# Selective-scan stage on one core: later split of B, B products and decays issued further ahead, one more decay buffer

## The chip, the cores and the metric

One NeuronCore of a Trainium2 chip runs the whole kernel. The metric is device time in microseconds (us) for one execution; lower is better. The engines are named as in the profile: PE is TensorE (matmuls), DVE is VectorE, ACT is ScalarE, POOL is GpSimd and SP is the engine that issues most DMAs.

## What is computed

The program is a Mamba block (layer norm, input projection, short convolution, selective scan in both directions, gate, output projection) on 4 images of 96 channels and 1024 positions, followed by a windowed-attention block with an MLP. The change is in the first part. Cut to what it touches:

```python
dbl = xr @ W_xproj
dt = jax.nn.softplus(dbl[..., :DT_RANK] @ W_dt + b_dt)
Bm = dbl[..., DT_RANK:DT_RANK + D_STATE]
Cm = dbl[..., DT_RANK + D_STATE:]
A = -jnp.exp(A_log)
def step(h, inp):
    dt_t, B_t, C_t, x_t = inp
    h = jnp.exp(dt_t[:, :, None] * A) * h + (dt_t * x_t)[:, :, None] * B_t[:, None, :]
    y_t = jnp.einsum('ben,bn->be', h, C_t)
    return (h, y_t)
```

There are 192 inner channels, 16 states, 1024 steps and 8 sequences (4 images in 2 directions).

## The kernel before, in words

The (sequence, channel) pairs fill 12 tiles of 128 partitions. Each tile has 16 **units**, one for each state, so the stage has 192 units, and unit k is state k mod 16 of tile k // 16. A unit takes these steps, each on a [128, 1024] fp32 array:

- ScalarE makes the decay `a = exp(dt*A)` (`decay(k)`, L620) into a ring of `A_RING` buffers.
- B of this state is spread over the channels. For 165 units TensorE does it with matmuls into PSUM (`spread_b`, L421), and VectorE multiplies the result by `u = dt*x` (`times_b`, L789). For the 27 units of `POOL_UNITS` a DMA replicates B into `b_rep`, GpSimd multiplies it by `u` (`b_product`, L759), and ScalarE copies the product to PSUM (`copy_b`, L630).
- VectorE runs the recurrence over the 1024 steps (`scan`, L802).
- GpSimd multiplies the states by C, which a DMA has replicated (`read_out`, L749, result `hc`).
- TensorE adds `hc` into the tile's output in PSUM by an identity matmul (`sum_states`, L451), three units later (`SUM_LAG`).

Every engine runs its own program in order; semaphores join them. The program of an engine is a loop over k, and at each k it also does what `front(k)` finds in the hand-written table `PLAN`: projections and convolutions for later tiles (jobs `conv`, `xp`, `dt`, `z`, `cen`, `var`, `out`), each with the unit at which TensorE issues it. TensorE has two PSUM banks `f_ps` for these jobs, so a job waits until ScalarE has emptied the bank of the job two before it. In step k TensorE spreads B for unit k + 1, then does `front(k)`, then sums unit k - 3. ScalarE in step k does `copy_b(k + 1)`, `decay(k + 2)` and `front(k)`; its copy and its decay of a step both wait for the scan of unit k - 1. GpSimd in step k does `b_product(k + B_AHEAD)`, `read_out(k)` and `front(k)`. The scan of unit k waits for the state product of unit k - 4, since the ring of states has four buffers.

The projection `xp` gives B and C for one sequence. B is needed by TensorE as three bf16 terms that add up to the fp32 value. They are made in a relay between two engines: ScalarE rounds to the high term (L543), GpSimd subtracts it (`rest`, L694), ScalarE rounds the remainder to the middle term (`middle`, L550 and L551), and GpSimd subtracts again (`lowest`, L700). There are eight sequences, of which one is split before the loop. The `dt` job has a relay as well: ScalarE takes four passes (`softplus`), then GpSimd does four operations in four successive units (`soft_lost`, `soft_more`, `soft_sum`, `dt_times_x`, L705 to L718). For images 2 and 3 the norm has one too: ScalarE, GpSimd (`scale_norm`, L686), ScalarE (`affine`, L518).

Of the kernel before, what the change touches and what calls it, by code (L numbers as in the profile page):

```python
# [18 lines left out]
E_LO, E_HI = 128, E_IN - 128  # L19
PAIR_ROWS = E_HI  # L20
LN_EPS = 1e-5
A_RING, H_RING, HC_RING, C_RING, SUM_LAG = 3, 4, 4, 4, 3
ROWS = 3 * 2 * N_ST + RANK
LOADS = [4, 7, 12, 8]

# [26 lines left out]
def cols(th, n=HALF):  # L52
# [38 lines left out]
SEQS = [j[1:3] for j in JOBS if j[0] == "xp" and j[3] == 0]  # L91
POOL_UNITS = (4, 18, 22, 36, 38, 46, 51, 53, 65, 68, 80, 83, 97, 99, 113, 117, 126, 130, 136, 147, 153, 163, 165, 177,
              181, 185, 189)
B_RING, B_AHEAD, B_LOAD = 2, 3, 3


def groups_of(b):
# [34 lines left out]
def mamba(nc, t, x1, early, bn_stats, bc_d):  # L132

    with ExitStack() as ctx:
        def sb(name, shape, dt=F32):
            return ctx.enter_context(nc.sbuf_tensor(name, shape, dt))
# [22 lines left out]
        var = sb("var", [C, L])  # L159
# [332 lines left out]
        def _(act):  # L492
# [17 lines left out]
            def variance_left(b, th):  # L510
                leave(("var", b, th), var[:, cols(th)], bank("var", b, th)[0:C, :], ACT.Ln, bias=norm[:, 2:3])
                if th == 1:
                    left(act, J("var", b, 1))
                    nc.scalar.activation(var[:, :], var[:, :], ACT.Exp, scale=-0.5).then_inc(inverse, 1)
# [6 lines left out]
            def conv_left(tile, th):  # L521
                if th == 0 and tile in XR_BEFORE:
                    act.wait_ge(summed, N_ST * XR_BEFORE[tile] + SKIP_UNIT + 2)
                leave(("conv", tile, th), xr_of(tile)[:, cols(th)], bank("conv", tile, th),
                      bias=conv_b[:, kind_of(tile):kind_of(tile) + 1])

            def silu(tile):
                left(act, J("conv", tile, 1))
                nc.scalar.activation(xr_of(tile), xr_of(tile), ACT.Silu).then_inc(xr_ready, 1)

            def xp_left(b, d, th):
                slot = seq_slot(b, d)
                if b >= 2 and th == 0:
                    act.wait_ge(c_stored[slot], 16)
                    act.wait_ge(st_done, SEQS.index((b - 2, d)) + 1)
                    act.wait_ge(job_done, J("dt", tile_of("H", 0, d), 1))
                leave(("xp", b, d, th), dbc[:, slot, cols(th)], bank("xp", b, d, th)[0:ROWS, :], ACT.Copy)
                if th == 1:
                    left(act, J("xp", b, d, 1))
                    act.dma_start(bc_d[2 * b + d], dbc[0:2 * N_ST, slot, :]).then_inc(c_stored[slot], 16)  # L540
                    if b >= 2:
                        act.wait_ge(spread, products_before(N_ST * (tile_of("H", 0, d) + 1)))
                    nc.scalar.activation(st[:, slot, :], dbc[0:ROWS - RANK, slot, :], ACT.Copy).then_inc(st_high, 1)  # L543

            def middle(b, d):
                slot, i = seq_slot(b, d), SEQS.index((b, d))
                act.wait_ge(st_rest, i + 1)
                if i:
                    act.wait_ge(st_done, i)
                nc.scalar.activation(st[64:96, slot, :], dbc[64:96, slot, :], ACT.Copy).then_inc(st_mid, 1)  # L550
                nc.scalar.activation(mid[0:32, :], dbc[0:32, slot, :], ACT.Copy).then_inc(st_mid, 1)  # L551

            def dt_left(tile, th):
                kind = kind_of(tile)
                if th == 0:
                    if tile:
                        act.wait_ge(soft, 4 * tile)
                    if tile >= 2:
                        act.wait_ge(exp_done, N_ST * (tile - 1))
                act.wait_ge(job_done, J("dt", tile, th))  # L560
                nc.scalar.activation(dt[:, tile % 2, cols(th)], bank("dt", tile, th), ACT.Relu,
                                     bias=b_dt[:, kind:kind + 1])
                nc.scalar.activation(t3[:, cols(th)], bank("dt", tile, th), ACT.Abs, bias=b_dt[:, kind:kind + 1])\  # L563
                    .then_inc(left_act, 1)
# [21 lines left out]
            def front(k):  # L586

                for at, name, *job in PLAN:
                    done = DONE_AT[(name, *job)]
                    if done == k and name == "conv":  # L590
                        conv_left(*job)
                        if job[1] == 1:
                            silu(job[0])
                    if done == k and name == "xp":
                        xp_left(*job)
                    if done + 2 == k and name == "xp" and job[2] == 1:
                        middle(*job[0:2])
                    if done == k and name == "dt":
                        dt_left(*job)
                    if done + 1 == k and name == "dt" and job[1] == 1:  # L600
                        softplus(job[0])
                    if done == k and name == "cen":
                        center_left(*job)
                    if done == k and name == "var":
                        variance_left(*job)
                    if done + 3 == k and name == "var" and job[1] == 1:
                        affine(job[0])
                    if done == k and name == "z":
                        z_left(*job)

            def decay(k):

                if k >= UNITS:
                    return
                tile, n = divmod(k, N_ST)
                if n == 0:
                    act.wait_ge(soft, 4 * tile + 3)
                if k >= A_RING:
                    act.wait_ge(scanned, k - A_RING + 1)
                nc.scalar.activation(a[:, k % A_RING, :], dt[:, tile % 2, :], ACT.Exp,  # L620
                                     scale=a_neg[:, kind_of(tile), n:n + 1]).then_inc(exp_done, 1)
# [51 lines left out]
            silu(1)  # L673
            nc.scalar.preload_act_table_set("natural_log_exp_and_others")
            act.wait_ge(set_up, 5)
            for k in range(2):
                decay(k)
            for k in range(UNITS):
                copy_y(k)
                copy_b(k + 1)  # L680
                decay(k + 2)
                front(k)

        def scale_norm(engine, eng, b):
# [35 lines left out]
        @block.gpsimd  # L720
        def _(pool):
            def front(k):

                for at, name, *job in PLAN:
                    done = DONE_AT[(name, *job)]
                    if name == "xp" and job[2] == 1:
                        if done + 1 == k:
                            rest(nc.gpsimd, pool, SEQS.index(tuple(job[0:2])))
                        if done + 2 == k:
                            lowest(nc.gpsimd, pool, SEQS.index(tuple(job[0:2])))  # L730
                    if name == "dt" and job[1] == 1:
                        if done + 2 == k:
                            soft_lost(nc.gpsimd, pool, job[0])
                        if done + 3 == k:
                            soft_more(nc.gpsimd, pool, job[0])
                        if done + 4 == k:
                            soft_sum(nc.gpsimd, pool, job[0])
                        if done + 5 == k:
                            dt_times_x(nc.gpsimd, pool, job[0])
                    if name == "var" and job[1] == 1 and done + 1 == k:  # L740
                        scale_norm(nc.gpsimd, pool, job[0])

            def read_out(k):

                pool.wait_ge(scanned, k + 1)
                pool.wait_ge(c_in[k % C_RING], 16 * c_loads(k))
                if k >= HC_RING:
                    pool.wait_ge(summed, k - HC_RING + 1)
                nc.gpsimd.tensor_tensor(hc[:, k % HC_RING, :], h[:, k % H_RING, :], c_rep[:, k % C_RING, :],  # L749
                                        ALU.mult).then_inc(hc_done, 1)  # L750

            def b_product(k):

                if k not in POOL_UNITS:
                    return
                i, tile = POOL_UNITS.index(k), k // N_ST
                pool.wait_ge(soft, 4 * (tile + 1))
                pool.wait_ge(b_in[i % B_RING], 16 * b_loads(i))
                nc.gpsimd.tensor_tensor(b_rep[:, i % B_RING, :], b_rep[:, i % B_RING, :], u[:, tile % 2, :],  # L759
                                        ALU.mult).then_inc(b_times_u, 1)  # L760

            for k in range(UNITS):
                b_product(k + B_AHEAD)
                if k < UNITS - 1:
                    read_out(k)
                front(k)
# [694 lines left out]
```

## Time and profile before

| | |
|---|---|
| time, median of 3 runs | 1193.46 us (1192.46 to 1195.16) |
| the profiled execution's own time | 1198.2 us |
| its span | 1196.4 us |
| busy over the span: PE, DVE, ACT, POOL | 90%, 77%, 48%, 77% |
| mean granted clock of TensorE | 0.944 of full speed |
| busy from 100 to 200 us: PE, DVE, ACT, POOL | 95.50, 93.59, 71.81, 98.33 us |

The units run from 60 to 750 us; the attention block fills the rest. Busy time counts an instruction from its start to its end, and neighbours on one engine overlap a little, so a row's mean is slightly longer than the step from one start to the next. In a timeline the bracket at the end of a row is the time that the engine stood idle before it, and what ended that.

### The profile page before, as it was taken

The page shows a single profiled execution, that of the slowest core. Times are in us where ns is not written, and L with a number is a line of the kernel's source. Part 1 is how long each engine was busy: PE and PEld are TensorE (multiplying, and loading weights), DVE is VectorE, ACT ScalarE, POOL GpSimd, SP SyncE. Part 2 cuts the span into 40 slices and gives each one's busy share as a digit, 9 for nine tenths or more (in the row PEclk, how much of TensorE's full clock was granted, in tenths as well). Part 3 has the DMA queues.
Part 4 walks back from the last instruction along what each step waited for, and adds up shares of the span by engine and source line. Part 5 has one row for each costly group of instructions (what it writes and reads, how often), then busy time and mean ns, then how long its engine had stood idle before and what let it go on. Part 6 is the DMA issues. An engine that isn't in the chain of part 4 may idle for free. (4 is left out here: it accounts for less than half of the span.)

```text
span 1196.4 us, 9538 instructions
## 1 busy us (share of the span) xinstructions
PE 1073.9 (90%) x3268; PEld 376.1 (31%) x3268; DVE 920.1 (77%) x598; ACT 572.2 (48%) x601; POOL 919.3 (77%) x371
## 2 busy tenths in 40 slices
PE   7889999799998999998987979699999999997675
PEld 2223333233333333333332323233333333332221
DVE  1299998779998899998989899400587796969871
ACT  5766858697777654867675644211121121011311
POOL 0089999979998979998999998100298877989880
PEclk8879999899999999999998999699999999998787
DMA  3234566544475545664546474343938476473402
GB/s 84 93 127 157 178 179 158 186 134 157 163 191 146 176 145 147 173 199 154 169 169 176 129 224 157 83 104 73 201 74 184 89 171 116 116 132 58 91 0 75
DMA packets 111042, 165.65 MB, mean 138 GB/s; under 512 B 63411, under 2 KB 76441, under 8 KB 110993
## 3 DMA queue, kind: packets, MB, share of 16 engines
q1 hardware_dynamic: 108880, 157.81, 48.9%
q10 hardware_dynamic: 2112, 7.23, 2.1%
q8 instruction: 26, 0.43, 0.1%
q14 instruction: 24, 0.19, 0.1%
HBM read 137.43 MB, written 11.23 MB: 124 GB/s over the span
## 5 line engine op out<-in xcount | busy, mean ns | idle before, releaser
L749 POOL TENSOR_TENSOR hc<-h,c_rep 128x1024 f32<-128x1024 f32 x191 | 447.5, 2359 | 103.4 <-DVE h L802 91.3
L802 DVE TENSOR_TENSOR_SCAN h<-a,bu 128x1024 f32<-128x1024 f32 x192 | 436.9, 2284 | 32.9 <-ACT bu L630 10.0
L451 PE MATMUL y_ps<-hc,ident 128*128 128x512 f32 x768 | 378.4, 617 | 0.8 <-DVE hc L850 0.3
L620 ACT ACTIVATE a<-dt,a_neg 128x1024 f32<-128x1024 f32 x192 | 216.5, 1143 | 132.1 <-DVE h L802 126.9
L1231 POOL TENSOR_TENSOR prod_p<-vw,at 128x3584 f32<-128x3584 f32 x18 | 130.4, 7242 | 122.8 <-DMA vw<-v_d 116.9
L789 DVE TENSOR_TENSOR bu<-bu,u 128x1024 f32<-128x1024 f32 x165 | 199.7, 1210 | 21.9 <-PE bu L421 21.7
L451 PEld LDWEIGHTS y_ps<-hc,ident 128*128 128x128 f32 x768 | 144.5, 195 | 202.9 <-issue 182.1
L1112 PE MATMUL sc_ps<-x,w_up 128*64 128x512 f32 x672 | 177.9, 604 | 1.2 <-DMA x<-qk 1.2
L1112 PE MATMUL sc_ps<-x,w_low 96*64 96x512 f32 x672 | 177.5, 603 | 0.0
L1182 ACT ACTIVATE sc<-sc_ps,rel 128x512 f32<-128x512 f32 x24 | 16.5, 688 | 257.4 <-PE sc_ps L1112 257.4
L421 PE MATMUL bu<-st,pick 96*128 96x512 bf16 (+1 forms) x438 | 101.7, 390 | 37.8 <-DVE h L802 36.3
L1238 POOL TENSOR_TENSOR prod_p<-prod_p 128x1536 f32<-128x1536 f32 (+1 forms) x36 | 104.6, 2905 | 2.8
L1317 DVE TENSOR_REDUCE e_ps<-at 128x32 f32<-128x1568 f32 x6 | 17.5, 2921 | 98.1 <-DMA at<-scores_d 98.1
L1231 DVE TENSOR_TENSOR prod_v<-vw,e_ps 128x3584 f32<-128x3584 f32 (+1 forms) x24 | 86.8, 3616 | 0.5
L1337 DVE TENSOR_TENSOR acc_ps<-acc_ps,prod_v 128x1024 f32<-128x1024 f32 x66 | 81.3, 1232 | 2.3
L1112 PEld LDWEIGHTS sc_ps<-x,w_up 128*64 128x64 f32 x672 | 49.6, 137 | 101.4 <-issue 101.4
L1112 PEld LDWEIGHTS sc_ps<-x,w_low 96*64 96x64 f32 x672 | 49.8, 136 | 98.7 <-issue 98.7
L329 PE MATMUL f_ps<-xn,w_taps 96*128 96x512 f32 x128 | 70.4, 653 | 7.4 <-ACT t L563 5.2
L421 PEld LDWEIGHTS bu<-st,pick 96*128 96x128 bf16 (+1 forms) x438 | 26.7, 103 | 155.9 <-DVE h L802 84.4
L759 POOL TENSOR_TENSOR b_rep<-b_rep,u 128x1024 f32<-128x1024 f32 x27 | 63.6, 2357 | 2.8 <-DMA b_rep<-bc_d 2.8
L1128 PE MATMUL g_ps<-x,c_w 96*128 96x512 f32 x48 | 33.3, 855 | 25.5 <-DVE x L1309 25.5
L1204 ACT ACTIVATE up<-g_ps,c_b 128x512 f32<-128x512 f32 x24 | 16.5, 687 | 70.9 <-PE g_ps L1128 70.9
(130 smaller groups left out, 992.6 us busy)
## 6 DMA issues: line engine op xcount, KB each, us to landing
c_rep<-bc_d SPq DMA_DIRECT2D x128, 512.0 KB, 4.0
c_rep<-bc_d SPq DMA_DIRECT2D x128, 256.0 KB, 4.1
vw<-v_d SPq DMA_DIRECT2D x24, 532.0 KB, 9.1
x<-qk SPq DMA_DIRECT2D x66, 171.0 KB, 5.3
b_rep<-bc_d SPq DMA_DIRECT2D x17, 512.0 KB, 5.0
b_rep<-bc_d SPq DMA_DIRECT2D x20, 256.0 KB, 5.2
scores_d<-sc ACTq DMA_DIRECT2D x24, 196.0 KB
at<-scores_d SPq DMA_DIRECT2D x24, 196.0 KB, 3.4
```

The lines of the kernel that those rows point to most:

```text
L329: mm = pe.matmul(out, w_taps[:, j, 0:E_LO], xn[:, i, s:s + HALF], start=(j == 0), stop=(j == TAPS - 1))
L421: mm = pe.matmul(bu[rows, k % 2, cols(th)], pick[:, n:n + 1].to_broadcast([ROWS - RANK, rows.stop - rows.start]), st[:, seq_slot(b, d), co ...
L451: mm = pe.matmul(y_ps[:, cols(th)], ident[:, :], hc[:, k % HC_RING, cols(th)], start=(n == 0 and d == 0), stop=(n == N_ST - 1))
L620: nc.scalar.activation(a[:, k % A_RING, :], dt[:, tile % 2, :], ACT.Exp, scale=a_neg[:, kind_of(tile), n:n + 1]).then_inc(exp_done, 1)
L749: nc.gpsimd.tensor_tensor(hc[:, k % HC_RING, :], h[:, k % H_RING, :], c_rep[:, k % C_RING, :], ALU.mult).then_inc(hc_done, 1)
L759: nc.gpsimd.tensor_tensor(b_rep[:, i % B_RING, :], b_rep[:, i % B_RING, :], u[:, tile % 2, :], ALU.mult).then_inc(b_times_u, 1)
L789: nc.vector.tensor_tensor(bu[:, k % 2, :], bu[:, k % 2, :], u[:, tile % 2, :], ALU.mult)\
L802: nc.vector.tensor_tensor_scan(scan_order(h[:, k % H_RING, :], d), scan_order(a[:, k % A_RING, :], d), scan_order(bu[:, k % 2, :], d), 0.0 ...
L1112: mm = pe.matmul(sc_ps[64 * i:64 * i + 64, th, :], w[:, dx, :], x4[0:rows, (2 * p + i) % X4_RING, y:y + 16, dx:dx + W], start=(dx == 0 and ...
L1231: return engine.tensor_tensor(prod, shifted, e[:, lo:hi].unsqueeze(2).broadcast_to([128, hi - lo, HD, W]), ALU.mult)
L1238: nc.gpsimd.tensor_tensor(prod_p[:, lo[0]:lo[1]], prod_p[:, lo[0]:lo[1]], prod_p[:, hi[0]:hi[1]], ALU.add).then_inc(pp, 1)
L1337: nc.vector.tensor_tensor(acc_v, acc_v, prod_v[:, k:k + 2], ALU.add).then_inc(pv, 1)
```

## The change

Four numbers move. `middle` on ScalarE goes from 2 to 5 units after the end of its `xp` job, and `lowest` on GpSimd from 2 to 6 units after it; `rest` stays one unit after. `b_product` and the DMA load that feeds it go from 3 to 4 units ahead of their unit. The decay ring goes from 3 to 4 buffers, and step k makes the decay of unit k + 3 where it made that of k + 2, behind the same wait. `affine` goes from 3 to 4 units after its `var` job.

```diff
-A_RING, H_RING, HC_RING, C_RING, SUM_LAG = 3, 4, 4, 4, 3
+A_RING, H_RING, HC_RING, C_RING, SUM_LAG = 4, 4, 4, 4, 3
...
-B_RING, B_AHEAD, B_LOAD = 2, 3, 3
+B_RING, B_AHEAD, B_LOAD = 2, 4, 4
+MID_LAG, LOWEST_LAG = 5, 6
...
-                    if done + 2 == k and name == "xp" and job[2] == 1:
+                    if done + MID_LAG == k and name == "xp" and job[2] == 1:
                         middle(*job[0:2])
...
-                    if done + 3 == k and name == "var" and job[1] == 1:
+                    if done + 4 == k and name == "var" and job[1] == 1:
                         affine(job[0])
...
-            for k in range(2):
+            for k in range(A_RING - 1):
                 decay(k)
             for k in range(UNITS):
                 copy_y(k)
                 copy_b(k + 1)
-                decay(k + 2)
+                decay(k + A_RING - 1)
                 front(k)
...
-                        if done + 2 == k:
+                        if done + LOWEST_LAG == k:
                             lowest(nc.gpsimd, pool, SEQS.index(tuple(job[0:2])))
```

ScalarE's program before, from the copy for unit 46 on. L550 and L551 are `middle` of the sequence whose `xp` job ends at unit 44; L496 with `z` empties the bank of a `z` job:

```order
L630 ACTIVATE bu<-b_rep 128x1024
L620 ACTIVATE a<-dt,a_neg 128x1024
L496 ACTIVATE z<-f_ps 128x512
L620 ACTIVATE a<-dt,a_neg 128x1024
L550 ACTIVATE st<-dbc 32x1024
L551 ACTIVATE mid<-dbc 32x1024
L496 ACTIVATE z<-f_ps 128x512
L584 ACT_TABLE_LOAD
L584 ACTIVATE z<-z 128x1024
```

The same place in the changed kernel, whose lines are one or two higher, up to the copy for unit 51:

```order
L497 ACTIVATE z<-f_ps 128x512
L585 ACT_TABLE_LOAD
L585 ACTIVATE z<-z 128x1024
L621 ACT_TABLE_LOAD
L621 ACTIVATE a<-dt,a_neg 128x1024
L497 ACTIVATE xn<-f_ps 96x512
L509 ACTIVATE var<-xn 96x512
L621 ACTIVATE a<-dt,a_neg 128x1024
L551 ACTIVATE st<-dbc 32x1024
L552 ACTIVATE mid<-dbc 32x1024
L631 ACTIVATE bu<-b_rep 128x1024
```

The middle term now stands behind the second `z` bank and two `cen` banks, directly ahead of the copy for unit 51.

GpSimd's program before, from the B product for unit 46 on (the next two B products are for units 51 and 53; L694 is `rest`, L700 `lowest`, L686 `scale_norm`):

```order
L759 TENSOR_TENSOR b_rep<-b_rep,u 128x1024
L749 TENSOR_TENSOR hc<-h,c_rep 128x1024 x3
L694 TENSOR_TENSOR dbc<-dbc,st 96x1024
L749 TENSOR_TENSOR hc<-h,c_rep 128x1024
L700 TENSOR_TENSOR st<-dbc,mid 32x1024
L749 TENSOR_TENSOR hc<-h,c_rep 128x1024
L759 TENSOR_TENSOR b_rep<-b_rep,u 128x1024
L749 TENSOR_TENSOR hc<-h,c_rep 128x1024 x2
L759 TENSOR_TENSOR b_rep<-b_rep,u 128x1024
L749 TENSOR_TENSOR hc<-h,c_rep 128x1024 x3
L686 TENSOR_TENSOR xn<-xn,var 96x1024
```

And in the changed kernel:

```order
L760 TENSOR_TENSOR b_rep<-b_rep,u 128x1024
L750 TENSOR_TENSOR hc<-h,c_rep 128x1024 x4
L695 TENSOR_TENSOR dbc<-dbc,st 96x1024
L750 TENSOR_TENSOR hc<-h,c_rep 128x1024
L760 TENSOR_TENSOR b_rep<-b_rep,u 128x1024
L750 TENSOR_TENSOR hc<-h,c_rep 128x1024 x2
L760 TENSOR_TENSOR b_rep<-b_rep,u 128x1024
L750 TENSOR_TENSOR hc<-h,c_rep 128x1024 x2
L701 TENSOR_TENSOR st<-dbc,mid 32x1024
L750 TENSOR_TENSOR hc<-h,c_rep 128x1024 x2
L687 TENSOR_TENSOR xn<-xn,var 96x1024
```

Each B product has gone ahead of one more state product, and `lowest` has gone behind both B products.

GpSimd's program at units 5 to 10 before (L705 and L709 are the first two operations of the `dt` relay, `soft_lost` and `soft_more`):

```order
L694 TENSOR_TENSOR dbc<-dbc,st 96x1024
L749 TENSOR_TENSOR hc<-h,c_rep 128x1024
L700 TENSOR_TENSOR st<-dbc,mid 32x1024
L749 TENSOR_TENSOR hc<-h,c_rep 128x1024 x3
L705 TENSOR_TENSOR t<-t,u 128x1024
L749 TENSOR_TENSOR hc<-h,c_rep 128x1024
L709 TENSOR_TENSOR t<-t 128x1024
```

And in the changed kernel:

```order
L695 TENSOR_TENSOR dbc<-dbc,st 96x1024
L750 TENSOR_TENSOR hc<-h,c_rep 128x1024 x4
L706 TENSOR_TENSOR t<-t,u 128x1024
L750 TENSOR_TENSOR hc<-h,c_rep 128x1024
L701 TENSOR_TENSOR st<-dbc,mid 32x1024
L710 TENSOR_TENSOR t<-t 128x1024
```

`lowest` has gone into the `dt` relay. It does so for five of the seven sequences that are split inside the loop (at units 10, 89, 107, 138 and 154; the other two are at 35 and 50).


## Rows read from the trace of the kernel before

**Rows 1.** The page: the span, and the busy time of each engine.
```profile
span 1196.4 us, 9538 instructions
...
PE 1073.9 (90%) x3268; PEld 376.1 (31%) x3268; DVE 920.1 (77%) x598; ACT 572.2 (48%) x601; POOL 919.3 (77%) x371
```

**Rows 2.** The page's costliest groups, the scan stage's own: busy, mean ns, idle before.
```profile
L749 POOL TENSOR_TENSOR hc<-h,c_rep 128x1024 f32<-128x1024 f32 x191 | 447.5, 2359 | 103.4 <-DVE h L802 91.3
L802 DVE TENSOR_TENSOR_SCAN h<-a,bu 128x1024 f32<-128x1024 f32 x192 | 436.9, 2284 | 32.9 <-ACT bu L630 10.0
...
L620 ACT ACTIVATE a<-dt,a_neg 128x1024 f32<-128x1024 f32 x192 | 216.5, 1143 | 132.1 <-DVE h L802 126.9
...
L789 DVE TENSOR_TENSOR bu<-bu,u 128x1024 f32<-128x1024 f32 x165 | 199.7, 1210 | 21.9 <-PE bu L421 21.7
```

**Rows 3.** Busy time per engine from GpSimd's first to its last state product.
```profile
62.36:748.80 686.44, 629.38 (x1648) 227.71 (x1648) 629.16 (x366) 459.61 (x464) 641.83 (x278) 0.97 0.54 165
221.00:266.20 45.20, 36.68 (x81) 14.19 (x80) 31.01 (x19) 38.68 (x43) 37.37 (x17) 0.89 0.46 163
```

**Rows 4.** Waits of VectorE from 60 to 720 us: total, times, longest.
```profile
DVE bu L789 <- PE bu L421: 20.9, 14, 7.1
DVE h L802 <- ACT bu L630: 10.0, 5, 3.7
DVE h L802 <- ACT a L620: 8.1, 5, 2.4
```

**Rows 5.** Waits of ScalarE from 60 to 720 us, the two that name GpSimd.
```profile
ACT st L550 <- POOL dbc L694: 27.6, 7, 5.4
...
ACT bu L630 <- POOL b_rep L759: 18.0, 8, 5.0
```

**Rows 6.** Timelines of ScalarE, TensorE, VectorE and GpSimd, units 46 to 55.
```profile
226.42 1.05 ACT L550 ACTIVATE st<-dbc 32x1024 bf16<-32x1024 f32 x1 [5.39 <-POOL dbc L694]
...
250.70 1.00 ACT L630 ACTIVATE bu<-b_rep 128x1024 f32<-128x1024 f32 x1
...
229.09 2.02 PE L313 MATMUL f_ps<-x,center 96*96 96x512 f32 x2 [5.79 <-ACT z L496]
...
235.26 1.23 DVE L789 TENSOR_TENSOR bu<-bu,u 128x1024 f32<-128x1024 f32 x1 [7.11 <-PE bu L421]
...
251.79 2.29 DVE L802 TENSOR_TENSOR_SCAN h<-a,bu 128x1024 f32<-128x1024 f32 x1 [3.75 <-ACT bu L630]
...
259.82 1.23 DVE L789 TENSOR_TENSOR bu<-bu,u 128x1024 f32<-128x1024 f32 x1 [2.24 <-PE bu L421]
...
266.20 2.37 POOL L705 TENSOR_TENSOR t<-t,u 128x1024 f32<-128x1024 f32 x1
```

**Rows 7.** Timelines of ScalarE and VectorE, units 85 to 90.
```profile
369.46 1.05 ACT L550 ACTIVATE st<-dbc 32x1024 bf16<-32x1024 f32 x1 [3.37 <-POOL dbc L694]
...
377.24 1.23 DVE L789 TENSOR_TENSOR bu<-bu,u 128x1024 f32<-128x1024 f32 x1 [1.83 <-PE bu L421]
...
385.38 1.23 DVE L789 TENSOR_TENSOR bu<-bu,u 128x1024 f32<-128x1024 f32 x1 [1.03 <-PE bu L421]
```

**Rows 8.** Timelines of ScalarE, VectorE and GpSimd, units 134 to 156.
```profile
548.34 1.05 ACT L550 ACTIVATE st<-dbc 32x1024 bf16<-32x1024 f32 x1 [4.48 <-POOL dbc L694]
...
552.61 2.29 DVE L802 TENSOR_TENSOR_SCAN h<-a,bu 128x1024 f32<-128x1024 f32 x1 [2.93 <-ACT bu L630]
...
556.67 1.23 DVE L789 TENSOR_TENSOR bu<-bu,u 128x1024 f32<-128x1024 f32 x1 [1.78 <-PE bu L421]
...
621.61 2.29 DVE L802 TENSOR_TENSOR_SCAN h<-a,bu 128x1024 f32<-128x1024 f32 x1 [1.90 <-ACT a L620]
...
626.93 2.29 DVE L802 TENSOR_TENSOR_SCAN h<-a,bu 128x1024 f32<-128x1024 f32 x1 [1.91 <-ACT a L620]
...
550.56 2.12 POOL L700 TENSOR_TENSOR st<-dbc,mid 32x1024 bf16<-32x1024 f32 x1
```

**Rows 9.** Timeline of VectorE, the scan of unit 38.
```profile
192.18 2.29 DVE L802 TENSOR_TENSOR_SCAN h<-a,bu 128x1024 f32<-128x1024 f32 x1 [2.66 <-ACT bu L630]
```

## The prediction

> **What bounds the kernel now.** I read the page first. TensorE is busy for 90% of the span and VectorE and GpSimd for 77% each [rows 1], but that is a mean over two blocks. The costliest groups show who works in the scan stage: GpSimd's state products (2.36 us each), VectorE's scans (2.28 us) and products (1.21 us), ScalarE's decays (1.14 us) [rows 2]. So I cut the stage out, from GpSimd's first state product to its last: 686.44 us, in which GpSimd is busy for 641.83 us, VectorE and TensorE for 629 us, ScalarE for 460 us [rows 3]. GpSimd stands idle for 44.6 us and can't finish sooner than its work allows. That is the ceiling of any change that only moves waits; TensorE and VectorE have 57 us each.
>
> Then the waits. VectorE waits 20.9 us for TensorE's spread B, 10.0 us for ScalarE's copies and 8.1 us for decays [rows 4]. ScalarE, the engine with most spare time, waits 27.6 us in seven stalls for `rest` and 18.0 us for B products [rows 5]. An idle ScalarE costs nothing by itself, so the timeline has to say what is queued behind the stall. At unit 46 it can be read off in full [rows 6]. ScalarE stands 5.39 us in front of `middle`. Behind that instruction is the emptying of a `z` bank; TensorE's next job needs the bank and stands 5.79 us; behind that job is the spread for unit 49, and VectorE stands 7.11 us. ScalarE then works without a gap until the copy for unit 53 starts at 250.70, and VectorE has stood another 3.75 us for it. So one late middle term holds three engines. The same pattern is at units 87 to 90 [rows 7] and 134 to 137 [rows 8].
>
> **The change part by part.** No instruction is added or taken away, so every term is a wait that goes or comes.
>
> *Middle term, first place (units 46 to 55).* `rest` is issued at unit 45 as before; `middle` is now in step 49, three units of 3.5 us after the point where ScalarE stalled, so the 5.39 us go. ScalarE has the same instructions from there to the copy for unit 53 (`middle` moves within that stretch), so the copy starts near 245.3 and scan 53 is 5.4 us earlier. That is the lower value. The upper one is GpSimd's idle time in this place: 45.20 us less 37.37 us busy, 7.8 us [rows 3]; VectorE can't win more for long, since its states must be taken away. Between them lies the wait of 2.24 us for TensorE at unit 55 [rows 6]. TensorE's two matmuls after the 5.79 us stall take 2.02 us, and its mean granted clock from 221.00 to 266.20 is 0.89 [rows 3], so it ran part of this place at the lower level, 1.2 GHz, and came late at unit 55. I take the upper value, because the delayed spreads go too. **-7.8 us.**
> The Trainium skill (TensorE: Matmul & The Clock Gate, the section on HAM oscillation) says that idle gaps of TensorE send its clock down and that the cure is to close the gaps. The trace agrees in that the slow pair follows a stall of 5.79 us. By the page the clock stays up once the stall is gone, and the term is 7.8 us; if the clock fell here all the same, it would be 5.4 us.
>
> *Second place (units 85 to 90).* `middle` would stand in step 88, and the `dt` banks are emptied 3.4 us earlier, so the waits of 1.83 and 1.03 us go [rows 7]. **-2.9 us.**
>
> *Third place (units 134 to 156).* The stall of 4.48 us goes, and with it VectorE's 2.93 and 1.78 us. At 621.61 and 626.93 VectorE waits 1.90 and 1.91 us for decays [rows 8]: ScalarE is in `softplus` and `z` and makes decay k + 2 only after them. With the fourth buffer it is one unit (3.5 us) ahead, which covers both. Sum 8.5 us. GpSimd, where `lowest` takes 2.12 us [rows 8], can't follow all of it: `lowest` moves into the relay at units 138 and 154, and I let it take 2.8 us back. **-5.7 us.**
>
> *The other small waits.* The waits for spread B not named so far are 20.9 - 7.11 - 2.24 - 1.83 - 1.03 - 1.78 = 6.9 us in nine places [rows 4, 6 to 8]. Most come where TensorE has a job in each unit, which the change leaves. **-1.0 us**, ends 0 and -6.9.
>
> *B products a unit earlier.* ScalarE's 18.0 us of waits for them [rows 5] mostly go. What hid them is the second `bu` buffer, and VectorE's 10.0 us for copies are 3.75 and 2.93 (counted above), 2.66 (unit 38) and 0.7. The load also goes a unit earlier, so its distance to the product is unchanged: 0.
>
> *Unit 38, against.* VectorE waits 2.66 us for a copy [rows 9] which stands behind `softplus` on ScalarE. Nothing in the change takes that away. `middle` of the sequence before it moves from unit 31 to unit 34, directly ahead of these crowded units, with two instructions of 1.05 us each. About half is covered by ScalarE's slack there. **+0.9 us**, ends 0 and +2.1.
>
> *GpSimd's lag, against.* Each unit costs VectorE 1.21 + 2.28 = 3.5 us and GpSimd 2.36 us, and each operation of a relay, or a B product, another 2.37 us [rows 2, 6]. In four relay units GpSimd falls 4 x (4.7 - 3.5) = 4.8 us behind; with `lowest` inside it is 7, and with a B product, which also takes 1.2 us from VectorE's unit, over 10. The ring of four states allows 4 x 3.5 - 2.28 - 2.36 = 9.4 us. Before, `lowest` came two or three units ahead of the relay and part of it fell into idle time. Five relays are now longer; I charge one `lowest`. **+2.1 us**, ends 0 and +10.5.
>
> *Fourth buffer and `affine`.* At a tile's first decay ScalarE now waits for `soft_sum` one unit earlier, up to 5 us. Behind it stand decays that VectorE needs two or three units later and, at those units, no bank: 0. If that cover were gone, each of the 11 tiles would cost up to one GpSimd operation, 2.4 us. `affine` is covered in the same way, by the units until its convolution.
>
> The sum is -7.8 - 2.9 - 5.7 - 1.0 + 0.9 + 2.1 = -14.4 us. It is made against the profiled execution, 1198.2 us with a span of 1196.4 us. That lies 4.7 us above the median of the runs, and nothing in the terms depends on the difference: 1193.46 - 14.4 = 1179 us.
>
> **The rivals.**
> *Forecast, 0.50:* the three places open up; 1174 to 1184 us.
> *GpSimd takes over, 0.20.* It is busy for 641.83 of 686.44 us [rows 3], and the waits of VectorE for ScalarE turn into waits for state products. Then only the first place pays, where GpSimd itself was idle, in part: 5.4 us, less one `lowest` of 2.1, which is 1190; 1185 to 1191 us. For it: the load is balanced to 2%. Against: in 221.00 to 266.20 GpSimd is idle for 7.8 us.
> *All of it opens up, 0.15.* If nothing is given back, the terms without the two losses and the 2.8 us give 20.2 us, and the rest of the 6.9 us and the clock may add some: 1166 to 1173 us. GpSimd's 44.6 us bound it.
> *No change, 0.08.* The stall was cover for something else, for instance a `z` or `cen` job whose data comes no sooner; ScalarE stands at the next instruction: 1191.5 to 1195.5 us.
> *Slower, 0.07.* One mechanism: GpSimd with `lowest` inside the relay. If its lag passes 9.4 us in all five, VectorE and, through the late sums, TensorE stop each time: 5 x 2.1 = 10.5 us, and the B products that now stand ahead of a tile's last state product (83, 99 and 163) delay three gates by up to 2.37 us, 7.1 us. With the 0.9 of unit 38 that is a loss of 18.5 us against gains of 17.4 us, about level. It turns into a loss when the third place, where this lag is largest, fails to open as well: 18.5 - 11.7 = 6.8 us, 1200 us.
>
> **How the numbers follow.** A measurement of this kernel can tell about 0.2% (2.4 us) from no change. Faster by more than that are the first three cases: 0.50 + 0.20 + 0.15 = 0.85. Within it 0.08, slower 0.07. The range leaves out the slower case and most of the unchanged one, 0.13, and the end of the open one: 1169 to 1191 us. The likeliest case alone has 1174 to 1184.
>
> **What the profile after would show.** If I am right: no stall of ScalarE for `rest` at all; no wait of VectorE above 3 us around units 49 and 136; the two waits for decays at units 155 and 156 gone; the granted clock near 1 from unit 46 to 55; GpSimd's busy time in the stage unchanged at 642 us in a stage of about 672 us. Wrong: VectorE's waits for spread B keep their sum with GpSimd's state product as the late end (GpSimd took over); the copy for unit 38 or 53 is late by more than before (`middle` sits badly in steps 34 and 49); waits of TensorE for `hc` grow at units 10 to 14, 89 to 92 or 107 to 110 (the lag). The attention block should not move.

## The result, and the profile after

| | before | changed |
|---|---|---|
| median | 1194.31 us (1192.46 to 1196.44, 4 runs) | 1177.50 us (1174.76 to 1178.73, 4 runs) |
| profiled execution | 1198.2 us, span 1196.4 us | 1174.8 us, span 1173.0 us |
| ratio of the times | | 0.9856, 95% interval 0.983 to 0.9881 |

The changed kernel is 1.4% faster; the forecast was 1179 us with a range of 1169 to 1191. The two profiled executions differ by 23.4 us, more than the medians do (16.8 us): before's lies 3.9 us above its median and the changed kernel's 2.7 us below. So each place below is read from the traces, and the size of the whole from the medians. Both traces have their first scan at 60.0 us.

The page of the changed kernel, to be held against [rows 1] and [rows 2]:

```profile
span 1173.0 us, 9538 instructions
...
PE 1067.1 (91%) x3268; PEld 373.3 (32%) x3268; DVE 919.6 (78%) x598; ACT 571.4 (49%) x601; POOL 919.5 (78%) x371
...
L803 DVE TENSOR_TENSOR_SCAN h<-a,bu 128x1024 f32<-128x1024 f32 x192 | 436.6, 2283 | 25.7 <-ACT bu L631 7.2
...
L790 DVE TENSOR_TENSOR bu<-bu,u 128x1024 f32<-128x1024 f32 x165 | 199.6, 1209 | 7.5 <-PE bu L422 5.7
```

The same instructions take the same time; the idle time before them has become less, for the scans from 32.9 to 25.7 us and for VectorE's products from 21.9 to 7.5 us. The next two rows cut out the scan stage in the same way as [rows 3], and the first place from the same time, 221.00 us, to the same instruction as there, the first of the `dt` relay on GpSimd:

```profile
62.36:727.03 664.67, 622.21 (x1648) 226.20 (x1648) 628.50 (x366) 458.62 (x464) 638.91 (x277) 0.98 0.55 171
221.00:258.63 37.63, 35.92 (x88) 13.88 (x87) 32.12 (x19) 37.23 (x41) 37.63 (x17) 0.95 0.56 193
```

The stage is 21.8 us shorter (686.44 to 664.67 us), with GpSimd's busy time within 0.5% of what it was. In the first place GpSimd is now busy for all of 37.63 us, where it had 7.8 us of idle time before. The waits of VectorE, ScalarE and TensorE from 60 to 700 us [rows 4, 5]:

```profile
DVE h L803 <- ACT bu L631: 7.2, 2, 3.9
...
DVE bu L790 <- PE bu L422: 4.9, 7, 1.9
DVE h L803 <- ACT a L621: 3.6, 3, 2.4
DVE bu L790 <- POOL u L719: 1.7, 2, 1.3
...
ACT a L621 <- POOL dt L714: 28.9, 5, 8.5
...
ACT bu L631 <- POOL b_rep L760: 12.5, 6, 3.2
...
PE y_ps L452 <- POOL hc L750: 15.7, 14, 2.1
```

The row of ScalarE for `rest` (27.6 us) is gone altogether, and VectorE's waits for spread B fell from 20.9 to 4.9 us. Three waits are new or much longer. ScalarE waits 28.9 us in front of a tile's first decay for `soft_sum`, where it was one wait of 2.4 us. VectorE waits 1.7 us for `u`, and TensorE waits 15.7 us for state products; neither stands in the list of before. The first place in the timelines of ScalarE, VectorE and GpSimd [rows 6]:

```profile
230.90 1.05 ACT L551 ACTIVATE st<-dbc 32x1024 bf16<-32x1024 f32 x1
231.98 1.06 ACT L552 ACTIVATE mid<-dbc 32x1024 bf16<-32x1024 f32 x1
232.94 1.00 ACT L631 ACTIVATE bu<-b_rep 128x1024 f32<-128x1024 f32 x1
...
244.66 1.01 ACT L631 ACTIVATE bu<-b_rep 128x1024 f32<-128x1024 f32 x1
...
245.75 2.29 DVE L803 TENSOR_TENSOR_SCAN h<-a,bu 128x1024 f32<-128x1024 f32 x1 [3.88 <-ACT bu L631]
...
252.09 1.23 DVE L790 TENSOR_TENSOR bu<-bu,u 128x1024 f32<-128x1024 f32 x1 [0.54 <-PE bu L422]
...
258.63 2.36 POOL L706 TENSOR_TENSOR t<-t,u 128x1024 f32<-128x1024 f32 x1
```

`middle` (L551, L552) runs without a stall, directly ahead of the copy for unit 51 (the third line). The copy for unit 53 starts at 244.66 where it started at 250.70, and scan 53 at 245.75. VectorE still waits 3.88 us for it. The relay on GpSimd starts at 258.63, before at 266.20: 7.6 us earlier.

### The profile page after: what moved, and what is told of

It is laid out like the page before. It is cut to its first block and busy times, and to the rows that moved or that the text cites. A ratio compares the mean times of both kernels' runs of the same rounds, so it can differ in the third digit from the quotient of the medians.

```text
span 1173.0 us, 9538 instructions
## 1 busy us (share of the span) xinstructions
PE 1067.1 (91%) x3268; PEld 373.3 (32%) x3268; DVE 919.6 (78%) x598; ACT 571.4 (49%) x601; POOL 919.5 (78%) x371
## 5 line engine op out<-in xcount | busy, mean ns | idle before, releaser
L803 DVE TENSOR_TENSOR_SCAN h<-a,bu 128x1024 f32<-128x1024 f32 x192 | 436.6, 2283 | 25.7 <-ACT bu L631 7.2
L452 PE MATMUL y_ps<-hc,ident 128*128 128x512 f32 x768 | 373.6, 610 | 16.2 <-POOL hc L750 15.8
L452 PEld LDWEIGHTS y_ps<-hc,ident 128*128 128x128 f32 x768 | 141.8, 192 | 218.0 <-issue 170.3
L760 POOL TENSOR_TENSOR b_rep<-b_rep,u 128x1024 f32<-128x1024 f32 x27 | 64.4, 2384 | 55.9 <-DVE u L719 54.1
```

The source lines that it names most:

```text
L452: mm = pe.matmul(y_ps[:, cols(th)], ident[:, :], hc[:, k % HC_RING, cols(th)], start=(n == 0 and d == 0), stop=(n == N_ST - 1))
L803: nc.vector.tensor_tensor_scan(scan_order(h[:, k % H_RING, :], d), scan_order(a[:, k % A_RING, :], d), scan_order(bu[:, k % 2, :], d), 0.0 ...
```

## The experiments

Each kernel was timed in alternation with the kernel before on one chip. A ratio is to the kernel before on the same chip, so kernels from different chips are compared by their ratios. In the traces the first scan starts anywhere from 55.9 to 60.4 us, with no relation to the edit (55.93 with B products earlier, 59.95 with the decay ring, 60.00 and 60.44 in two traces of the changed kernel). So a place is compared from scan to scan, and not by its time from the start of the trace.

### The parts of the change by themselves

The lags (how many units after its `xp` job `middle` and `lowest` come) alone, on the kernel before:

```diff
+MID_LAG, LOWEST_LAG = 5, 6
```

> The kernel before with one part of the change: the middle term 5 units and the lowest term 6 units after the end of the xp job. Decay ring 3, B products 3 ahead, affine 3. Theory 'stall' (ScalarE standing in front of the middle term holds the banks behind it): nearly all of the gain, 10 to 14 us off before; only VectorE's two waits of 1.9 us for decays at units 155 and 156 stay. Rival 'run-ahead' (the fourth decay buffer and the earlier B products make the gain, since they let ScalarE get ahead): at most 4 us off before.

Measured 1180.47 us against 1192.65, ratio 0.9901 (0.9883 to 0.9919), 12 us. The waits of VectorE:

```profile
DVE h L803 <- ACT bu L631: 9.0, 4, 5.1
DVE h L803 <- ACT a L621: 8.3, 6, 4.1
```

The sum for decays has not fallen (8.1 us before): the wait at unit 155 went and the one at unit 156 grew from 1.9 to 4.1 us. That is what this part leaves to the next one.

The decay ring alone:

```diff
-A_RING, H_RING, HC_RING, C_RING, SUM_LAG = 3, 4, 4, 4, 3
+A_RING, H_RING, HC_RING, C_RING, SUM_LAG = 4, 4, 4, 4, 3
```

> The kernel before with the fourth decay buffer and nothing else. Theory 'stall': the waits for decays go (8.1 us in the trace of before, of which 2.4 us is the first unit's), the stall and the chains of units 49, 88 and 136 stay: 2 to 5 us off before. Rival 'run-ahead': 8 us or more off before.

Measured 1188.05 us, ratio 0.9967 (0.9954 to 0.998), 4.6 us by the medians. ScalarE's stalls for `rest` and VectorE's long wait behind the first of them stand as before, and the waits for decays fall from 8.1 to 2.9 us:

```profile
ACT st L551 <- POOL dbc L695: 27.6, 7, 5.4
...
DVE bu L790 <- PE bu L422: 18.6, 13, 7.1
...
DVE h L803 <- ACT a L621: 2.9, 3, 2.2
```

B products and their loads a unit earlier, alone:

```diff
-B_RING, B_AHEAD, B_LOAD = 2, 3, 3
+B_RING, B_AHEAD, B_LOAD = 2, 4, 4
```

> The kernel before with B products and their loads 4 units ahead and nothing else. Theory 'stall': ScalarE's 18.0 us of waits for B products become small, VectorE gains nothing by it, within 2 us of before. Rival 'run-ahead': 3 to 6 us off before. A third possibility, since three of the 27 products now stand ahead of a tile's last state product: up to 3 us slower.

Measured 1192.73 us, ratio 1.0002 (0.9988 to 1.0015): no change. ScalarE's 18.0 us of waits for B products are gone from its list. The three parts together make 12.2 + 4.6 - 0.1 = 16.7 us by their medians, and the whole change 16.8 us. By the ratios it is 15.5 against 17.2 us, and the ratios have intervals of 1.5 to 3 us to either side. So the parts account for the change within these limits; a share of 2 or 3 us for their interplay or for `affine`, the fifth number that moves, which was not tried alone, is not excluded.

### The stall, one place at a time and in the other direction

Late lags for one sequence alone, on the kernel before (only the set differs between the two kernels):

```diff
+LATE = ((1, 1),)
...
-                    if done + 2 == k and name == "xp" and job[2] == 1:
+                    if name == "xp" and done + (5 if tuple(job[0:2]) in LATE else 2) == k and job[2] == 1:
...
-                        if done + 2 == k:
+                        if done + (6 if tuple(job[0:2]) in LATE else 2) == k:
```

> The kernel before, with the later lags (5 and 6) for one sequence alone, the one whose xp job ends at unit 44; the other six stay at 2 and 2, and ring, B products and affine are as before. Theory 'stall': the term of the first place alone, 6 to 8 us off before (the prediction said 7.8), with the waits at units 49 and 55 gone and the stalls at 88 and 136 in place. Rival 'spread out' (each place gives only what its own GpSimd idle time allows later on, so one place alone gives little): under 3 us.

Measured 1185.15 us against 1191.68, ratio 0.9949 (0.9931 to 0.9966), 6 us for one moved pair of operations. In the timeline of VectorE the wait of 7.11 us is gone and that for the copy has grown from 3.75 to 5.5 us, since ScalarE has the same instructions ahead of the copy and works them off almost without a gap:

```profile
DVE h L803 <- ACT bu L631: 11.5, 4, 5.5
DVE bu L790 <- PE bu L422: 10.5, 14, 1.8
```

With `LATE = ((2, 1),)`:

> The kernel before, with the later lags for the sequence whose xp job ends at unit 132 alone. Theory 'stall': the waits of 2.93 and 1.78 us at units 136 and 137 go, 4 to 5 us off before. If the longer dt relay (lowest at unit 138) takes it back: 2 us or less, with waits of VectorE for u or of TensorE for state products between units 139 and 146.

Measured 1188.41 us, ratio 0.9969 (0.9958 to 0.998), 3.7 us against the 4.7 us of the two waits. Both waits are gone from its trace, with none for `u` between units 139 and 146.

The dose the other way, `middle` a unit earlier than before (the numbers are used in the same lines as in the change; 2 and 2 is the kernel before):

```diff
+MID_LAG, LOWEST_LAG = 1, 2
```

> The kernel before with the middle term one unit EARLIER than before (1 unit after the end of the xp job, in the step in which GpSimd starts rest), nothing else. Theory 'stall': each of the seven stalls of ScalarE grows by up to a unit (3.5 us), total from 27.6 to about 45 to 52 us, and VectorE and TensorE wait for what is behind: 4 to 15 us slower than before. Rival (ScalarE's stall is cover, the gain comes from somewhere else): within 2 us of before.

Measured 1209.08 us, ratio 1.0148 (1.0124 to 1.0173), 17 us slower, a little more than expected. ScalarE's stalls, and the four longest waits in VectorE's timeline:

```profile
ACT st L551 <- POOL dbc L695: 49.3, 7, 8.0
...
237.23 1.23 DVE L790 TENSOR_TENSOR bu<-bu,u 128x1024 f32<-128x1024 f32 x1 [9.74 <-PE bu L422]
...
387.06 1.23 DVE L790 TENSOR_TENSOR bu<-bu,u 128x1024 f32<-128x1024 f32 x1 [4.55 <-PE bu L422]
...
429.98 1.23 DVE L782 TENSOR_TENSOR y<-y_ps,z 128x1024 f32<-128x1024 f32 x1 [5.63 <-PE y_ps L452]
...
459.18 0.69 DVE L774 SCALAR_TENSOR_TENSOR x<-f_ps,x 96x512 f32<-96x512 f32 x1 [6.73 <-PE f_ps L386]
```

The seven stalls grew from 27.6 to 49.3 us, by 21.7 us, and 17 us of that arrive in the time, where taking away 27.6 us of stalls gave 12 us. So with more of the same stall, less of it is covered. The wait at 459.18 is for a block of the output projection, after a stall of 7.14 us of ScalarE: other jobs behind the stalled ScalarE are late too, not spread B alone.

### How far the split has to move

The changed kernel with shorter lags, at which `lowest` stays ahead of all `dt` relays:

```diff
-MID_LAG, LOWEST_LAG = 5, 6
+MID_LAG, LOWEST_LAG = 3, 4
```

> The changed kernel, but with the middle term 3 and the lowest term 4 units after the end of the xp job (5 and 6 in the change). The lowest term then stands ahead of the dt relay at all seven places. Theory 'stall': one unit (3.5 us) of distance takes away most of each stall (3.4 to 5.4 us), so the time is that of the changed kernel, within 3 us. Rival 'GpSimd lag' (the lowest term inside the relay costs 2 us or more at each of five places): 3 us or more faster than the changed kernel. If distance is needed in full: 4 us or more slower than the changed kernel.

Measured 1175.64 us, ratio 0.9852 (0.9834 to 0.9869), the same as the changed kernel's 0.9856. ScalarE's waits:

```profile
ACT a L621 <- POOL dt L714: 22.4, 4, 7.2
...
ACT st L551 <- POOL dbc L695: 5.8, 4, 2.7
```

One unit of distance takes the stalls from 27.6 to 5.8 us. Two more units only remove the rest. By the time, a `lowest` inside the relay costs no more in all than those 5.8 us of stalls do (unit by unit, see the point on GpSimd's lag below). The large new wait, for `soft_sum`, is there with both lags.

### The largest waits that are left

VectorE still waits for two copies, at units 38 and 53. The changed kernel with lags 3 and 4 and these products on other units:

```diff
-POOL_UNITS = (4, 18, 22, 36, 38, 46, 51, 53, 65, 68, 80, 83, 97, 99, 113, 117, 126, 130, 136, 147, 153, 163, 165, 177,
+POOL_UNITS = (4, 18, 22, 36, 39, 46, 49, 51, 65, 68, 80, 83, 97, 99, 113, 117, 126, 130, 136, 147, 153, 163, 165, 177,
```

> The changed kernel with lags 3 and 4, and with GpSimd's B products of units 38 and 53 moved to units 39 and 49 (still 27). VectorE's largest waits left in the changed kernel, 3.3 us at unit 38 and 3.9 us at unit 53, are for ScalarE's copy of the product, which stands behind softplus and behind the variance job's table loads. If ScalarE's order is what costs there, the copies now stand ahead of or clear of that work: 3 to 7 us off the kernel with lags 3 and 4. If GpSimd's lag at these units is the limit, VectorE's wait only moves: within 2 us of it.

Measured 1177.67 us against 1191.68, ratio 0.99 (0.9871 to 0.9929): not faster. The profiled execution took 1187.67 us, 10 us above the median of its kernel, so only single places are read from its trace. VectorE's timeline:

```profile
193.57 2.29 DVE L803 TENSOR_TENSOR_SCAN h<-a,bu 128x1024 f32<-128x1024 f32 x1 [1.62 <-ACT bu L631]
...
217.13 2.29 DVE L803 TENSOR_TENSOR_SCAN h<-a,bu 128x1024 f32<-128x1024 f32 x1 [0.27 <-POOL hc L750]
...
232.64 2.29 DVE L803 TENSOR_TENSOR_SCAN h<-a,bu 128x1024 f32<-128x1024 f32 x1 [5.90 <-ACT bu L631]
```

The wait at unit 38 shrank to 1.62 us, now at unit 39, and a new one of 5.90 us stands at unit 49: its copy stands behind a middle term which waits for `rest`, and GpSimd is far behind here (9.7 us after the scan of unit 47). At 217.13 VectorE waits for a state product itself, which it nowhere does in the kernel before.

The same units with lags 5 and 6:

> The changed kernel (lags 5 and 6) with the B products of units 38 and 53 moved to 39 and 49. With lags 3 and 4 the same move brought a new wait of 5.9 us at unit 49, whose copy stood behind a stalled middle term while GpSimd was 9.7 us behind. With lag 5 the middle term comes after that copy. If that stall was what spoiled it: 2 to 5 us off the changed kernel. If GpSimd's lag is the limit by itself: no faster than the changed kernel, with waits of VectorE for state products near unit 46.

Measured 1175.21 us, ratio 0.9846 (0.9821 to 0.9871), 1.6 us below the changed kernel on the same chip, within the intervals. The wait at unit 49 is gone, and waits of up to 2.3 us stand at units 39, 42, 51 and 53. Two of its six executions took 1170.0 and 1170.3 us.

Two products fewer on GpSimd, lags 5 and 6:

```diff
-POOL_UNITS = (4, 18, 22, 36, 38, 46, 51, 53, 65, 68, 80, 83, 97, 99, 113, 117, 126, 130, 136, 147, 153, 163, 165, 177,
+POOL_UNITS = (4, 18, 22, 36, 46, 51, 65, 68, 80, 83, 97, 99, 113, 117, 126, 130, 136, 147, 153, 163, 165, 177,
```

> The changed kernel with 25 B products on GpSimd, those of units 38 and 53 given back to TensorE and VectorE. VectorE gets two products (2.6 us), loses the waits for the two copies (3.3 and 3.9 us), and GpSimd has 4.7 us less to do. If the copies behind ScalarE's work are a cost of their own: 2 to 6 us off the changed kernel. If VectorE's work is the bound: 2 us slower or the same.

Measured 1169.84 us against 1192.17, ratio 0.9817 (0.9799 to 0.9834), 7 us below the changed kernel on the same chip; its five executions lie between 1169.50 and 1171.59 us. The waits of VectorE for copies are gone; those for spread B grew by 5 us:

```profile
DVE bu L790 <- PE bu L422: 9.7, 14, 1.9
...
DVE h L803 <- POOL hc L750: 1.0, 2, 0.6
```

The changed kernel beside it:

> The changed kernel again, beside the two others on this chip: its ratio to the kernel before should be within 0.3% of the 0.9856 that was measured first.

Measured 1176.80 us, ratio 0.9863 (0.9842 to 0.9885).

The traces do not show where the 7 us are. These are the stretches from the first scan to the start of the last, in the kernel with 25 products:

```profile
55.94:722.05 666.11, 619.44 (x1653) 224.89 (x1653) 632.87 (x368) 459.11 (x464) 633.54 (x275) 0.98 0.55 169
```

and in the repeat of the changed kernel:

```profile
60.44:725.14 664.70, 620.95 (x1646) 225.43 (x1647) 629.45 (x366) 461.17 (x466) 637.92 (x277) 0.98 0.55 171
```

VectorE gains 4.2 us at units 38 and 53 and gives 5.9 us back at units 55, 56, 103, 104 and 126 to 137, so the stage is not shorter (666.1 us against 664.7). The trace is 4.9 us shorter because its first scan starts 4.5 us earlier, where the edit has not acted yet, and the block behind the stage is 1.9 us shorter. How the other four executions divide is not recorded, so how much of the 7 us belongs to the two copies stays open.

And the control, with two other products given back:

```diff
-POOL_UNITS = (4, 18, 22, 36, 38, 46, 51, 53, 65, 68, 80, 83, 97, 99, 113, 117, 126, 130, 136, 147, 153, 163, 165, 177,
+POOL_UNITS = (4, 18, 22, 36, 38, 46, 51, 53, 65, 68, 80, 83, 97, 99, 113, 117, 136, 147, 153, 163, 165, 177,
```

> A control for the kernel with 25 B products: the changed kernel with two other products given back, those of units 126 and 130, for which VectorE does not wait in the changed kernel; 38 and 53 stay. GpSimd has the same 4.7 us less to do and VectorE the same 2.6 us more. If the gain of giving back 38 and 53 (7 us off the changed kernel) came from the two waits for copies: 1 us faster to 3 us slower than the changed kernel here. If it came from GpSimd's load as such: 4 us or more faster here as well.

Measured 1176.71 us against 1192.88, ratio 0.9873 (0.9851 to 0.9895): no gain over the changed kernel. VectorE's waits:

```profile
DVE bu L790 <- PE bu L422: 8.0, 10, 2.2
DVE h L803 <- ACT bu L631: 7.2, 2, 3.9
```

The 7.2 us for copies stand, as in the changed kernel. From its first scan to its last the trace takes 671.7 us, 5.5 us more than with units 38 and 53 given back. So less work for GpSimd as such is worth nothing here; which units are given back matters. Whether at 38 and 53 it is the late copy or GpSimd's load just there that counts, the two runs do not tell apart.

## Why the prediction was right, point by point

**What bounds the stage.** That ScalarE, half idle, sets the pace through what is queued behind its stall is shown three ways: the lags alone bring 12 of the 16.8 us, one sequence alone brings 6, and an earlier `middle` costs 17. The rival that ScalarE's stall was cover is out with the last of these.

The table gives each term as forecast, and how far scans of the changed kernel moved against the same scans of before between two units, from the two traces. Minus is earlier, in us.

| term | forecast | traces | where |
|---|---|---|---|
| first place | -7.8 | -8.8 | units 48 to 55 |
| second place | -2.9 | -2.7 | units 83 to 90 |
| third place, less GpSimd's share | -8.5 + 2.8 | -9.6 + 3.7 | units 128 to 163 |
| other small waits | -1.0 | -1.4 | units 9 and 72 |
| unit 38 | +0.9 | +0.7 | |
| GpSimd's lag elsewhere | +2.1 | +1.0 | unit 23 |
| not named | 0 | -4.4 | -2.2 at units 99 to 105, -2.1 at unit 166 |

The rows make -21.5 us of the 21.8; the rest are steps below 1 us, the largest +0.7 at unit 67, of which 0.6 us come with the earlier B products alone as well. The forecast of the sum, -14.4 us, is met by the medians (-16.8 us) and not by the traces: against them it is 7.4 us short (see *Not named* below).

**First place.** The copy for unit 53 came 6.0 us earlier and the relay 7.6 us, between my ends of 5.4 and 7.8 us. VectorE's own scans moved by 8.8 us, since VectorE came into the place 1.05 us late (units 23 and 38) and GpSimd only 0.4 us; GpSimd's idle time of 7.8 us did cap the gain, for none of it is left. By itself the place gives 6.1 us by the times (4.0 to 8.2 from the interval), so the upper end was the right choice only within the whole change. My reason for it, that the clock stays up, does not hold: it fell again in this place (last section), and the term was reached all the same. The other reason, that the delayed spreads go, holds: the wait at unit 55 went from 2.24 to 0.54 us.

**Third place.** The waits behind the stall and the two for decays went (-9.6 us from unit 128 to 156), and GpSimd took some back, 3.7 us between units 137 and 163, where I had let it take 2.8. The form of it was new: VectorE stands for `u` at the tile's start (in the repeat of the changed kernel at most 0.3 us of it), and the gate at unit 162 is later. These are from the timeline of VectorE:

```profile
564.54 1.23 DVE L790 TENSOR_TENSOR bu<-bu,u 128x1024 f32<-128x1024 f32 x1 [1.32 <-POOL u L719]
...
610.06 2.29 DVE L803 TENSOR_TENSOR_SCAN h<-a,bu 128x1024 f32<-128x1024 f32 x1 [0.70 <-ACT a L621]
...
619.68 1.23 DVE L790 TENSOR_TENSOR bu<-bu,u 128x1024 f32<-128x1024 f32 x1 [0.34 <-POOL u L719]
...
630.98 1.23 DVE L782 TENSOR_TENSOR y<-y_ps,z 128x1024 f32<-128x1024 f32 x1 [0.69 <-PE y_ps L452]
```

**Decays.** The ring alone gives 4.6 us by medians (the interval of the ratio makes it 2.4 to 5.5), its waits 5.2 us. I had booked 3.8 us of that inside the third place. Right in mechanism and size. (The waits for decays include one of 2.4 us at unit 0, which stays with the ring.)

**B products earlier.** Forecast 0, measured 0 (-1.4 to +1.8 us). ScalarE's waits for the products are idle time of an engine that nobody waits for there. That they would mostly go holds only for this part alone: in the changed kernel 12.5 of the 18.0 us are left.

**GpSimd's lag.** Right in sum, only in part for the reason given. I charged 2.8 us inside the third place and 2.1 us beside it, 4.9 us; the traces show 3.7 and 1.0, 4.7 us. The reason was `lowest` inside the relay, and at two units it is. In the changed kernel `lowest` is in the relay before unit 16, the last operation of the relay ends later, and VectorE stands longer at unit 23 (GpSimd twice, then VectorE):

```profile
99.74 2.12 POOL L701 TENSOR_TENSOR st<-dbc,mid 32x1024 bf16<-32x1024 f32 x1
...
111.05 2.36 POOL L719 TENSOR_TENSOR u<-dt,xr 128x1024 f32<-128x1024 f32 x1
...
137.91 1.23 DVE L790 TENSOR_TENSOR bu<-bu,u 128x1024 f32<-128x1024 f32 x1 [1.95 <-PE bu L422]
```

With lags 3 and 4 `lowest` is ahead of the relay, where GpSimd had idle time, and the wait is what it was before, 0.90 us:

```profile
91.27 2.13 POOL L701 TENSOR_TENSOR st<-dbc,mid 32x1024 bf16<-32x1024 f32 x1
...
109.54 2.35 POOL L719 TENSOR_TENSOR u<-dt,xr 128x1024 f32<-128x1024 f32 x1
...
136.52 1.23 DVE L790 TENSOR_TENSOR bu<-bu,u 128x1024 f32<-128x1024 f32 x1 [0.90 <-PE bu L422]
```

This 1.0 us, and 0.4 us at unit 160, are in all five traces with lags 5 and 6 and the other parts, and in neither of the two with lags 3 and 4. With the lags alone neither is there, so it takes the other parts as well. The rest of the loss is not due to the position. The largest part, at unit 144 (1.4 us, 0.4 us in the repeat), is also 1.4 us in the trace with lags 3 and 4, and it is gone where the products of units 126 and 130 were taken off GpSimd: there GpSimd's whole load costs, against a VectorE that is no longer held up. The small steps at units 149, 157 and 163 were not tested. The kernel with lags 3 and 4 is no faster all the same, since it loses against the changed kernel elsewhere (1.2 us at unit 153, 0.7 us at unit 90). Nor did the ring limit of 9.4 us come into play in the changed kernel. It did, a little, with lags 3 and 4 and with 25 products (VectorE waited 0.8 and 1.0 us for state products), and where units 39 and 49 were used: there GpSimd got 9.7 us behind at unit 47.

**Fourth buffer at a tile's start.** I wrote up to 5 us for ScalarE's wait for `soft_sum` and no cost. The size was wrong: it is up to 8.45 us, 28.9 us in five waits:

```profile
108.81 3.23 ACT L621 ACTIVATE a<-dt,a_neg 128x1024 f32<-128x1024 f32 x3 [7.53 <-POOL dt L714]
...
559.92 1.15 ACT L621 ACTIVATE a<-dt,a_neg 128x1024 f32<-128x1024 f32 x1 [8.45 <-POOL dt L714]
```

The cover held: VectorE's waits for decays are 3.6 us in all, 2.4 us of them at unit 0. So ScalarE's waits are now longer in sum at this place than the 27.6 us of stalls were, and cost next to nothing; the stalls of before were harmful by what stood behind them.

**Not named.** At units 99 to 105 and at 166 VectorE waited for TensorE before, in stretches where the granted clock was at its lower level, 1.2 GHz. In the changed trace the level was up there; in the traces with the ring alone and with one place alone the wait at unit 166 is 0 to 0.5 us as well. It is 0 with the B products alone too, which change nothing in the time. So 2.1 us of the 21.8 between the traces most likely belong to the one profiled execution of before, not to the change, and so do 0.6 us at unit 119 and 0.4 us at unit 126, which went with one place alone and with the B products alone as well. Of the 2.2 us at units 99 to 105, the 1.5 at units 103 and 104 came again in the repeat of the changed kernel and in no other trace; what makes them was not tested.

**The signs.** No stall for `rest` is left, the waits at units 155 and 156 are gone, and the attention block did not move (its TensorE is busy for 395 of its last 446 us in both traces). The clock was not near 1 in the first place (0.95 from 221.00 to 258.63), and a wait of 3.9 us stays at unit 53. Two of the signs of being wrong showed, at a small price: the waits for the copies of units 38 and 53 grew, from 2.66 and 3.75 to 3.3 and 3.88 us, and TensorE waits 15.7 us for state products, though never in the three stretches that I named. That wait comes with the parts together: it is 0.5 us with the lags alone and 1.8 us with the ring alone.

**The rivals.** Of "GpSimd takes over" the part is true that GpSimd is now nearest to its limit: it has 26 us of idle time left in the stage, half of it ahead of 110 us and behind 640 us. But two products fewer, at units 126 and 130, brought nothing. "All of it opens up" needed 1166 to 1173 us, and the kernel with 25 products gets there by its median, by an edit that the change does not contain.

## What to carry to other kernels

An engine that is busy for half its time can still set the pace: look for what stands behind its longest wait in program order, here a PSUM bank that two other engines needed, and move the waiting instruction back in the program by the time its input is late (one unit sufficed here; three were no better). Sum such gains per place from the waits in the timeline, but cap each with the idle time of the most loaded engine in the same place. Once the stall is gone, try taking back offloaded work whose result is picked up late: here taking back two of 27 products measured 7 us less and taking back two others nothing, though the traces leave open how much of the 7 us is theirs.

## What the runs showed of the hardware

TensorE's granted clock fell to its lower level without a long stall of TensorE. In the changed kernel's first place, busy times and clock in two stretches and TensorE's timeline between them:

```profile
228.00:238.00 10.00, 9.31 (x23) 3.27 (x22) 9.82 (x6) 9.87 (x12) 10.00 (x5) 1.00 0.49 185
238.40:241.80 3.40, 3.40 (x5) 1.35 (x5) 3.31 (x2) 3.36 (x4) 3.40 (x2) 0.50 0.17 55
...
236.25 0.61 PE L422 MATMUL bu<-st,pick 96*128 96x512 bf16 x2 [0.46 <-DVE h L803]
237.07 1.12 PE L360 MATMUL f_ps<-dbc,w_dt 6*128 6x512 f32 x2 [0.22 <-ACT var L497]
238.12 3.57 PE L441 MATMUL y_ps<-y,ident 128*128 128x512 f32 x4
```

TensorE was busy for 9.31 of the 10 us ahead of it and its pauses there are 0.46 and 0.22 us, yet from 238.4 to 241.8 the clock is at 0.50, and four matmuls take 3.57 us (1.98 at full clock). So closing the gaps raised the mean clock of the stage from 0.97 to 0.98 and of the first place from 0.89 to 0.95, but did not end such stretches.

The Trainium skill (TensorE: Matmul & The Clock Gate, the section on HAM oscillation) says that idle gaps of TensorE send its clock down and that the cure is to close them. For this place the trace does not agree: the stall was closed and the clock fell. The measurement decides.
